# The second quantised pass of an eight-stage block: the sigmoid's quantisation on GpSimd, one eviction on VectorE

## The reference

```
x    = act_qdq(layernorm(x))                        # 16 bits, one scale for the tensor
up   = act_qdq(x @ lpbq_dequant(w_up).T)            # 128 -> 384
gate = act_qdq(x @ lpbq_dequant(w_gate).T)          # 128 -> 384
sig  = fixed_qdq_u16(sigmoid(gate))                 # clip(round(65536 * s), 0, 65535) / 65536
gate = act_qdq(gate * sig)
o    = act_qdq(gate * up)
return o @ lpbq_dequant(w_down).T
```

## Time and profile before

| what | us |
|---|---|
| median of three runs (2119.83 to 2121.06) | 2120.57 |
| profiled execution, own time | 2123.0 |
| its span, first to last instruction | 2121.2 |
| second pass within it | 1910 to 1997 |
| TensorE busy over the whole span | 1897.6 (89%) |
| VectorE | 1669.4 (79%) |
| ScalarE | 1295.0 (61%) |
| GpSimd | 257.2 (12%) |

### The profile page before, as it was taken

How to read it: one execution, slowest core, us unless ns; L and a number is a source line. 1 busy time by engine, 2 the same in 40 slices (tenths; PEclk the granted TensorE clock), 3 DMA queues, 4 the chain that set the end, 5 groups by cost and what they waited for, 6 DMA issues and landing times.

```text
span 2121.2 us, 47279 instructions
## 1 busy us (share of the span) xinstructions
PE 1897.6 (89%) x17713; PEld 1447.9 (68%) x17713; DVE 1669.4 (79%) x4756; ACT 1295.0 (61%) x3167; POOL 257.2 (12%) x551
## 2 busy tenths in 40 slices
PE   7999999999969989999989796999999993799608
PEld 5787887787759987878767574677677772344208
DVE  6787787787859969999957796777876498787894
ACT  5777777787752328888856464554455266108744
POOL 1111111111101111111111142000000023000000
PEclk9999999999979989999989898999999997899859
DMA  5222221111126631111100012322322120002452
GB/s 154 54 67 61 52 58 43 45 46 45 42 77 242 237 108 32 32 32 32 30 1 2 15 56 77 98 82 91 106 92 82 51 60 12 0 0 116 182 178 80
DMA packets 123395, 152.32 MB, mean 72 GB/s; under 512 B 45817, under 2 KB 98594, under 8 KB 121122
## 3 DMA queue, kind: packets, MB, share of 16 engines
q1 hardware_dynamic: 119986, 147.71, 22.5%
q10 hardware_dynamic: 3184, 1.58, 0.3%
HBM read 110.19 MB, written 22.28 MB: 62 GB/s over the span
## 4 chain that ended last, share of the span: by engine, by line
PE 68%; DVE 14%; DMA 6%; ACT 5%; issue 3%; POOL 2%; SPq 2%; POOLq 0%; ACTq 0%; DVEq 0%
PE banks L1638 7%; PE banks L1648 7%; PE banks L488 5%; PE banks L1955 4%; PE banks L527 4%; PE banks L477 3%; PE banks L1054 3%; PE banks L1114 3%; PE banks L1280 3%; PE banks L861 3%; PE banks L533 3%; PE banks L1289 3%; PE banks L500 2%; DMA arena<-arena 2%; PE banks L508 2%
## 5 line engine op out<-in xcount | busy, mean ns | idle before, releaser
L1813 ACT ACTIVATE arena<-banks,b1c 128x512 f32<-128x512 f32 x192 | 131.5, 687 | 141.7 <-PE banks L1638 140.1
L1742 DVE TENSOR_TENSOR arena<-arena 128x512 f32<-128x512 f32 (+1 forms) x256 | 170.4, 687 | 55.5 <-ACT arena L1813 48.4
L612 ACT ACTIVATE arena<-banks,arena 128x128 f32<-128x128 f32 x512 | 180.7, 373 | 1.2 <-DVE arena L559 1.2
L1648 PEld LDWEIGHTS banks<-w2a,arena 128*128 128x128 f32 x1024 | 122.0, 192 | 20.1 <-issue 20.1
L488 PE MATMUL banks<-arena,wk 128*128 128x128 f32 x1024 | 134.1, 285 | 1.5 <-DVE arena L583 1.5
L527 PE MATMUL banks<-wv,arena 128*128 128x512 f32 x256 | 131.0, 594 | 0.0
L488 PEld LDWEIGHTS banks<-arena,wk 128*128 128x128 f32 x1024 | 121.8, 195 | 12.7 <-issue 10.8
L861 PE MATMUL banks<-we,arena 128*128 128x128 f32 x1024 | 127.6, 283 | 0.8 <-DVE arena L931 0.2
L1648 PE MATMUL banks<-w2a,arena 128*128 128x128 f32 x1024 | 124.7, 275 | 0.0
L861 PEld LDWEIGHTS banks<-we,arena 128*128 128x128 f32 x1024 | 121.1, 196 | 4.0 <-DVE arena L931 3.3
L1638 PE MATMUL banks<-arena,w1s 128*128 128x512 f32 x256 | 122.9, 614 | 0.0
(11 more groups left out here) (253 smaller groups left out, 4980.1 us busy)
## 6 DMA issues: line engine op xcount, KB each, us to landing
arena<-coef_scratch SPq DMA_DIRECT2D x32, 2048.0 KB, 8.2
arena<-arena SPq DMA_DIRECT2D x256, 64.0 KB, 2.0
gated_scratch<-arena SPq DMA_DIRECT2D x16, 768.0 KB, 3.2
arena<-gated_scratch SPq DMA_DIRECT2D x16, 768.0 KB, 4.2
arena<-z1T_scratch SPq DMA_DIRECT2D x128, 64.0 KB, 2.3
arena<-in_ctx_turned SPq DMA_DIRECT2D x32, 256.0 KB, 2.9
arena<-in_ctx SPq DMA_DIRECT2D x64, 64.0 KB, 2.1
z1T_scratch<-arena SPq DMA_DIRECT2D x64, 64.0 KB, 1.6
```

Of the source, the lines that this page charges most:

```text
L612: act.activation(prob[:, o, c * P:(c + 1) * P], ps[:, SCORES + o, c * P:(c + 1) * P], ACT.Exp, bias=low[:, o, c:c + 1], accum_out=total[:, ...
L1648: mm = pe.matmul(ps[:, OUT + g.par, j * D:(j + 1) * D], hT[g.par][:, c, j * P:(j + 1) * P], w, start=c == 0, stop=c == CHUNKS2 - 1)
L1742: dve.tensor_tensor(by_tile, by_tile, wide_coef[g.par][rows, e], ALU.mult).then_inc(s["scaled"].sem, 1)
L1813: act.activation(hT[g.par][:, c, :], ps[:, HID + c % NHID, :], ACT.Gelu, bias=k.b1c[:, c:c + 1])\
```

## The change

GpSimd gets a loop over the 16 groups that quantises `sig` into `sigq`, which now has two buffers; the second buffer lies in the first half of the tile `gin[0]`, which is otherwise used from the third pass on. VectorE no longer does this operation; in its place it evicts the third `up` bank of each group, one group ahead of its other work, and signals `upq_last`. ScalarE evicts only the first two `up` banks (`ON_ACT` = 2). TensorE waits for `upq` or `upq_last`, by the bank.

More of the change, by code:

```diff
@@ L1861, in quantised3 @@
     k.taken = mark
-    gq, sig, sigq = [half(W) for _ in range(2)], [k.take(W) for _ in range(2)], k.take(W // 2).bitcast(U16)
+    gq, sig, sigq = [half(W) for _ in range(2)], [k.take(W) for _ in range(2)], [k.take(W // 2).bitcast(U16)]
     gs = [k.take(W) for _ in range(2)]
     gin = [k.take(W)]
+    sigq.append(gin[0][:, 0:W // 2].bitcast(U16))
+    ON_ACT = CHUNKS3 - 1
     k.taken = turned
@@ L1884, in quantised3 @@
     s = k.sigs(G, dict(
-        shift=2, xhs=GROUP, xmax=1, xq=1, xd=1, t_psum=1, xdT=1, p_psum=2 * CHUNKS3, pmax=2 * CHUNKS3, c_psum=2 * CHUNKS3, upq=CHUNKS3,
+        shift=2, xhs=GROUP, xmax=1, xq=1, xd=1, t_psum=1, xdT=1, p_psum=2 * CHUNKS3, pmax=2 * CHUNKS3, c_psum=2 * CHUNKS3, upq=ON_ACT, upq_last=1,
         gq=CHUNKS3, sig=1, sigq=1, gs=1, gsmax=1, gq2=1, prod=1, omax=1, oq=1, of=1, y_psum=1))
@@ L1980, in second @@
         def second(at):
+            def freed(b, n, c):
[5 more added lines that the diff above has]
+                    pe.wait_ge(*s["upq_last"](b))
             if g := at(0):
-                project(pe, g, s["c_psum"],
-                        lambda b, n, c: pe.wait_ge(*s["gq" if n else "upq"](b, c + 1)))
+                project(pe, g, s["c_psum"], freed)
         pe.wait_ge(*s["pmax"].all(G))
@@ L2050, in second @@
                     dve.wait_ge(*gs_stored(g.back(2)))
-                dve.scalar_tensor_tensor(out=gs[g.par], in0=gq[g.par], scalar=scale["ug"][:, 1:2], in1=sigq, op0=ALU.mult,
+                dve.scalar_tensor_tensor(out=gs[g.par], in0=gq[g.par], scalar=scale["ug"][:, 1:2], in1=sigq[g.par], op0=ALU.mult,
                                          op1=ALU.mult).then_inc(s["gs"].sem, 1)
```

## The result

The changed kernel takes 2161.28 us (median of 4 runs, 2157.56 to 2163.75), the kernel before 2120.20 beside it: 1.0186 times as long (95% interval 1.0168 to 1.0203), +41 us between the medians. The forecast was 2122.0 in a range up to 2125. The prediction was wrong, by its largest open price and on the side of the rival that it gave 0.11.

A forecast was written before the change was run, and what follows sets the result against it. The prediction took TensorE to bound the second pass's body, leaving only the tail exposed: +1.54 - 0.16 = +1.4 us, on the median 2120.57, gives 2122.0 us. The range was 2119.7 to 2125.

The forecast's parts named there:

- GpSimd gains the quantising: Second pass, each group: quantising 128x1536 float32 to uint16 on GpSimd was taken at 2.3 us, between 1.2 and 3.8.
- The high end: Quantising on GpSimd at most 3.8 us: three 128x512 additions with nothing taken off.
- the ends of the range: Low: quick and middle quantising cases with spread 0.7; high: 3.8 us without a lock (+2.9) and the same spread.
- the lock: Rival, second pass: GpSimd's quantising and VectorE's multiply exclude each other, loop becomes the bound; +11.6 us, 2132; chance 0.11.
- threshold of 3.2: Second pass: quantising and multiply fit into the 5.15 us period if quantising takes less than 5.15 - 1.93 = 3.2 us.
- TensorE bounded the body and ScalarE did not: Second pass: TensorE's 5.15 us per group hides ScalarE's saved eviction; rival, ScalarE bounds: -7.6 us, 2113, chance 0.04.
- VectorE's eviction was hidden: Second pass: VectorE's new PSUM eviction, taken at 0.69 us, fits under TensorE's 5.15 per group and costs nothing.
- The end of `gs` of group 15 moves everything behind it: End of second pass: whatever moves this end moves all that follows, including the third pass, by the same amount.
- The hops to and from GpSimd: Between sigmoid, quantising and multiply: 0.16 us to GpSimd and 0.11 back; with 2.3 of quantising, 2.57 instead of 1.03.
- the sum: Tail of the second pass: +1.54 us for the longer way through GpSimd, -0.16 for ScalarE's lost eviction, together +1.4.

The follow-up runs named there:

- The list: Kernel before, with GpSimd running scratch 128x1536 operations of several forms in the first pass, as two kernels; 2151.67 and 2154.48 us, one run each.
- 2.98 us: Changed kernel, but GpSimd quantises only the first 832 of 1536 columns with multiply-and-minimum; ratio 1.0016 to the kernel before.
- 1024 columns: Changed kernel, but GpSimd quantises only the first 1024 of 1536 columns with multiply-and-minimum; ratio 1.0029 to the kernel before.
- the run that takes turns: Changed kernel, but by a semaphore GpSimd waits for the multiply of group g-1 before quantising group g; ratio 1.0183 to the kernel before.
- VectorE's part alone: Kernel before, but VectorE evicts the third up bank one group ahead and also keeps the quantising, nothing on GpSimd; ratio 0.9998.
- the fast pair: Changed kernel, but GpSimd quantises with multiply-and-add-zero instead of multiply-and-minimum; ratio 1.0011 to the kernel before.
- the first price list: Kernel before, with GpSimd running scratch 128x1536 fills, scalar operations, copies and an addition, plus a 512-column quantising, in the first pass; one run.
- the run in chunks: Changed kernel with multiply-and-add-zero, and group 15's sigmoid, quantising and multiply in three 512-column pieces; ratio 0.9998 to the kernel before.

## Why the prediction was wrong

**The step that failed** is "GpSimd gains the quantising": 2.3 us, between 1.2 and 3.8. It measured 5.4. The bounds were drawn from a fill and an addition, as if GpSimd's price went by how many tiles it reads. The list shows that for this engine it goes by the form of the operation: the one-input pair multiply-minimum costs twice the two-input addition (2.75). No row at hand had the price of this pair: the two-scalar row on 4 columns (L711, 0.198) is a multiply and an add, the pair that turned out fast, and 4 columns say little of the price per column. But that the operation counts was there to be read: on the same 4 columns the power of two tiles (L714) takes 1.01 in the earlier trace rows, five times as long. The high end was not a bound, only the dearest row known, and it was written as one. The sentence from the Trainium skill ("GPSIMD Engine Reference", section "4.1 Engine selection") that one-input work runs roughly at line rate holds for copies and for multiply-add (1.46 to 1.53, near the estimate of 1.28 plus dispatch) and not for the form in the diff. A slip beside this changes nothing: by the terms given for them, the ends of the range would be 2120.2 (2120.57 + 0.3 - 0.7) and 2124.2 (2120.57 + 2.9 + 0.7), not 2119.7 and 2125.

**The rival that came true** is the lock, with a quantising past 3.2 us. Its threshold of 3.2 stands between two runs: 2.98 us costs nothing once the body is steady, 1024 columns (3.48) do. Its price worked out as quantising plus 1.93 gives 7.33 us per group at 5.4, and 7.41 was measured; 15 x (7.33 - 5.15) = 33 us against 34.1 of body. That the two are so close is partly luck. The rival has GpSimd wait for every multiply, and that is the loop of the run that takes turns (7.38). In the changed kernel a multiply in every third group waits for GpSimd instead, and ScalarE's evictions and sigmoid behind it, 3.57 us, happen to be as long as the two multiplies (3.64) that the rival counts in their place. The low chance given to the rival followed from the bound.

**What was right.** TensorE bounded the body and ScalarE did not: relieving ScalarE of one `up` eviction in three gave nothing with VectorE's part alone, nor with the fast pair, the two runs in which GpSimd was out of the way. VectorE's eviction was hidden (0.74 where 0.69 was taken). The end of `gs` of group 15 moves everything behind it: the third pass is shifted and otherwise nearly the same. The hops to and from GpSimd were taken at 0.16 and 0.11 and are 0.09 and 0.04 here. With the measured price and hops the sum comes out: +0.4 of tail with 1.47 us, +1.9 with 2.98.

## What to carry to other kernels

Before work goes to GpSimd, price the very form, the pair of operations included: here rewriting multiply-minimum as multiply-add made it 3.6 times faster. Then lay its interval beside VectorE's operations that read SBUF, the one with two tiles above all (the reduction was not held up here): if the two do not fit one after the other into the period, the period becomes about their sum. And relieving an engine that is busy all the time gains nothing when the engine that feeds it is the one with the longer period.

## What the runs showed of the hardware

A single operation on GpSimd is dearer than a multiply-add pair (4.14 against 1.5).

The shutting-out depends on who starts first. Beside a multiply already running GpSimd waits for its end: with 1024 columns each record ends 3.48 us after the multiply does, however early it started. The other way round the hold-up is shorter than GpSimd's record. In the changed kernel a multiply started just after a quantising of 1536 columns took 3.90 us longer than alone, not 5.4, and ended 0.30 after it (1934.72 and 1934.42). With 1024 columns a multiply started just after a quantising took only 0.87 longer than alone (2.69 in place of 1.82) and ended 0.99 before it (1966.14 and 1967.13). So by these records the multiply does not wait for the whole quantising; which part of it shuts the multiply out is not in the profile and stays open.

An operation with one SBUF input is held up as well, as in the earlier trace rows: in the first price list VectorE's scaling of 128x512 (L2062) took 5.47 us beside a quantising of 5.42. In the kernel before, where GpSimd rests in that pass, it takes 0.49 (L2039, the second row):

```profile
1823.80 5.47 DVE L2062 TENSOR_SCALAR xd<-xq,scale_x 128x512 f32<-128x512 int16 x1
...
L2039 DVE TENSOR_SCALAR xd<-xq,scale_x 128x512 f32<-128x512 int16 x16 | 7.8, 486 | 1.3 <-PE banks L1973 0.8
```

The first six matmuls of the second pass take 4.54 us in some executions and 2.84 in others, in different kernels: the mean granted clock is 0.76 from 1914.4 to 1921 in the run with the fast pair (partly the 1.2 GHz level) and 1.00 from 1915.4 to 1921 in the run in chunks, though TensorE had waited for the scale in both; why it differs stays open. The difference is 1.7 us, more than the tail's edits change, so those were read from the last matmul on.
